# A counter of passed waits on VectorE in a kernel of two transformer layers

## The chip, the cores and the metric

The kernel runs on one core of a Trainium2 chip. The metric is the device time of one execution in microseconds (us), median of three runs. The engines are TensorE (PE in the profile; PEld is its weight load), VectorE (DVE), ScalarE (ACT), GpSimd (POOL) and the DMA queues, of which SyncE (SP) issues most.

## The reference

Sixteen sequences of 256 rows of 128 channels pass through four sublayers. Each is `x = x + layernorm(sublayer(layernorm(x)))`:

```python
x = x + _layernorm(_L0_attn_ref(_layernorm(x), ...))  # a long convolution with a complex decaying filter
x = x + _layernorm(_L0_ffn_ref(_layernorm(x), ...))   # top 2 of 8 experts (softmax router) + a shared expert
x = x + _layernorm(_L1_attn_ref(_layernorm(x), ...))  # 16 heads of 64, causal, ALiBi, 2 null keys, l2-normed q and k
x = x + _layernorm(_L1_ffn_ref(_layernorm(x), ...))   # top 2 of 4 experts: SwiGLU, two MLPs, a small normed block
```

Mean and variance of rows are thus needed at ten or so places of a sequence, and each router needs the two largest of its logits:

```python
topk_probs, topk_idx = jax.lax.top_k(router_probs, TOP_K)   # L0_ffn
rw, sel = jax.lax.top_k(logits, K)                          # L1_ffn
```

## The kernel before

The sixteen sequences are worked in eight groups of two, that is four tiles of 128 rows. All data stay in SBUF; weights are loaded and folded in an opening. The work is a software pipeline: the letters in a step's name say which sublayer it belongs to, `e_` and the first part of `l_` the convolution, the rest of `l_` the first expert layer, `a_` the attention, `f_` the second expert layer. One round of the pipeline works on four groups at once (`MIDDLE`: e of group i+2, l of i+1, a of i, f of i-1), before it stand `PROLOGUE` and `FIRST`, behind it the shorter `LAST_L`, `LAST_A` and `LAST_F`. In each table the order of the steps on each engine is written out by hand, and each engine runs its list strictly in that order.

Engines meet through semaphores. A `Signal` is a semaphore that rises by a fixed number in each group, and `s.at(g, n)` is the value after n steps of group g. Every instruction that makes something raises its signal, and whoever needs it waits for the value; that holds inside one engine too: a DVE instruction that reads what the DVE instruction before it has written waits for its semaphore.

The steps that the text speaks of:

- `stats` and `half_stats` (L1297 and L1318) take mean and variance of four or two tiles on DVE: `bn_stats` for each tile, a wait for them, `bn_aggr` for each tile, a wait, and one `tensor_scalar` that makes `norm.var`. POOL then makes the reciprocal root (`root` L840, `half_root` L847: `rooted`), and DVE's `apply` or `half_apply` (L1310, L1332) normalizes the tiles; `half_residual` (L1338) adds the residual. The norms are n_x, n_y (convolution), n_l (router input), n_d (after the experts), n_a (before attention), n_o (after it), n_m (before the second expert layer), n_c, n_c2 (inside it), n_f (after it) and n_z (the same for the last group).
- `l_pick` (L1405) and `f_route` (L1559) copy the router's logits, take the eight largest of each row (`max`), wait, and take their places (`max_index`, in the trace MATCH_VALUE_LOAD and FIND_INDEX8).
- `l_xl` (L1386) makes `xaT_lo`, the low part of the attention's input, from PE's transposes; PE's first projection `a_m` (L1655 to L1657) needs it. In front of it PE runs `f_clock` (L1974), five matmuls whose result nobody reads.
- `l_cT` (PE, L1777) turns the routing coefficients; it also waits for `f_out` (DVE, L1607) of an earlier group, the weighted sum over the experts, which DVE runs behind `l_route`, `l_pick` and `l_coef`.
- `f_ceT` (PE, L1662) turns `ce_rows`, which DVE has normalized with n_c (L1310).
- `weigh_biases` (POOL, L900 and L904) and `conv_gains` (POOL, L856) are large element-wise operations of POOL.

A semaphore that is only counted up and that nobody waits for exists once already, in `keep_x2` on POOL: `pool.sem_inc(pool_passed, 1)` (L865). On DVE the opening has increments as instructions of their own, behind waits for DVE's own last result: `dve.sem_inc(z_made, 1)` (L1188), `dve.sem_inc(gain_made, 1)` (L1210) and others. There the helper `link` gives each instruction an increment of `made` and puts a wait for it behind it.

Of the kernel before, what the change touches and what calls it, by code (L numbers as in the profile page):

```python
# [228 lines left out]
def program(nc, a, out):  # L229
# [24 lines left out]
    with ExitStack() as ctx:  # L254
# [3 lines left out]
        def sem(name):  # L258
            return ctx.enter_context(nc.semaphore(name))
# [218 lines left out]


        last_stored = sem("last_stored")  # L480
        pool_passed = sem("pool_passed")

        x_loaded = signal("x_loaded", 16)
# [88 lines left out]
        def ce_and_logits(b):  # L572
            return bank[6 + b][:, 0:2 * (P + 8)].rearrange("p (t d) -> p t d", t=2)
# [55 lines left out]
        def tiles(h):  # L629
            return range(2 * h, 2 * h + 2)  # L630
# [539 lines left out]
        def _(dve):  # L1170
# [126 lines left out]
            def stats(norm, g, tile):  # L1297
                s = norm.steps
                for t in range(T):
                    V.bn_stats(norm.six[:, t, :], tile(t)).then_inc(s.sem, 1)  # L1300
                dve.wait_ge(s.sem, s.at(g, 4))
                for t in range(T):
                    V.bn_aggr(norm.mv[:, t, :], norm.six[:, t, :]).then_inc(s.sem, 1)
                dve.wait_ge(s.sem, s.at(g, 8))
                V.tensor_scalar(norm.var[:], norm.mv[:, :, 1], norm.scale, norm.add, ALU.mult, ALU.add).then_inc(s.sem, 1)
# [12 lines left out]
            def half_stats(norm, g, h, tile):  # L1318
                s = norm.steps[h]
                for t in tiles(h):  # L1320
                    V.bn_stats(norm.six[:, t, :], tile(t)).then_inc(s.sem, 1)
                dve.wait_ge(s.sem, s.at(g, 2))
                for t in tiles(h):
                    V.bn_aggr(norm.mv[:, t, :], norm.six[:, t, :]).then_inc(s.sem, 1)
                dve.wait_ge(s.sem, s.at(g, 4))
                V.tensor_scalar(norm.var[:, 2 * h:2 * h + 2], norm.mv[:, 2 * h:2 * h + 2, 1], norm.scale, norm.add,
                                ALU.mult, ALU.add).then_inc(s.sem, 1)
# [13 lines left out]
            def e_stats(g):  # L1341
                if first(g):
                    dve.wait_ge(x0_loaded, 16)
                else:
                    dve.wait_ge(x_loaded.sem, x_loaded.at(g))
                stats(n_x, g, lambda t: xin[:, t, :])
# [25 lines left out]
            def l_turn2(g):  # L1372
                dve.wait_ge(l_turned.sem, l_turned.at(g, 2))
                stats(n_y, g, lambda t: bank[3][:, t * P:(t + 1) * P])

            def l_res(g):
                apply(n_y, g, xn, lambda t: bank[3][:, t * P:(t + 1) * P])
                add_residual(n_y, g, x1, xn, xin)
                dve.wait_ge(n_y.steps.sem, n_y.steps.at(g))
                stats(n_l, g, lambda t: x1[:, t, :])  # L1380
# [24 lines left out]
            def l_pick_(g):  # L1405
                s = l_pick
                dve.wait_ge(s.sem, s.at(g, 1))
                for t in range(T):
                    V.max(top0[:, t, :], logit0[:, t, :]).then_inc(s.sem, 1)
                dve.wait_ge(s.sem, s.at(g, 1 + T))  # L1410
                for t in range(T):
                    V.max_index(idx0[:, t, :], top0[:, t, :], logit0[:, t, :]).then_inc(s.sem, 1)
                V.tensor_tensor(exp0[:], top0[:], top0[:, :, 0:1].to_broadcast([P, T, 8]), ALU.subtract).then_inc(s.sem, 1)
# [35 lines left out]
            def l_down_(g, h):  # L1449
                dve.wait_ge(l_down.sem, l_down.at(g, 2 * h + 2))  # L1450
                half_stats(n_d, g, h, lambda t: bank[4 + h][:, t * P:(t + 1) * P])
# [8 lines left out]
            def a_stats(g, h):  # L1460
                dve.wait_ge(n_d.steps[h].sem, n_d.steps[h].at(g))
                half_stats(n_a, g, h, lambda t: x2n[:, t, :])
# [57 lines left out]
            def a_out_(g, h):  # L1520
                dve.wait_ge(a_out.sem, a_out.at(g, h + 1))
                half_stats(n_o, g, h, lambda t: out_bank(g, h)[:, t * P:(t + 1) * P])
# [36 lines left out]
            def f_route(g):  # L1559
                s = f_pick  # L1560
                for b in range(2):
                    dve.wait_ge(f_ce.sem, f_ce.at(g, b + 1))
                    V.tensor_tensor(logit1[:, 2 * b:2 * b + 2, :], ce_and_logits(b)[:, :, P:P + 8],
                                    b1_router[:].unsqueeze(1).to_broadcast([P, 2, 8]), ALU.add).then_inc(s.sem, 1)
                dve.wait_ge(s.sem, s.at(g, 2))
                for t in range(T):
                    V.max(top1[:, t, :], logit1[:, t, :]).then_inc(s.sem, 1)
                dve.wait_ge(s.sem, s.at(g, 2 + T))
                for t in range(T):
                    V.max_index(idx1[:, t, :], top1[:, t, :], logit1[:, t, :]).then_inc(s.sem, 1)  # L1570
                V.tensor_tensor(gap1[:], top1[:, :, 1], top1[:, :, 0], ALU.subtract).then_inc(s.sem, 1)
# [58 lines left out]
            def f_end(g):  # L1630
# [6 lines left out]
                "s_null": s_null, "s_kvlo": s_kvlo, "s_qlo": s_qlo, "s_v2": s_v2, "s_bias": s_bias, "s_split": s_split,  # L1637
                "e_stats": e_stats, "e_apply": e_apply, "e_scan": e_scan, "e_sum": e_sum, "l_turn2": l_turn2, "l_res": l_res,
                "l_norm": l_norm, "l_turn3": l_turn3, "l_ct": l_cT, "l_xl": l_xl, "l_route": l_route, "l_pick": l_pick_, "l_coef": l_coef, "l_hg": l_hg_, "l_hu": l_hu_,
                "l_hc": l_hc_, "l_dstats": l_down_, "l_end": l_end, "l_astats": a_stats, "l_aapply": a_apply,  # L1640
                "a_null": a_null, "a_ss": a_sums, "a_u": a_units,
                "a_nexp": a_nexp_, "a_nt": null_low, "a_mix": a_mixes, "a_o": a_out_, "a_end": a_end,
                "f_stats": f_stats, "f_apply": f_apply, "f_route": f_route, "f_pick": f_pick_, "f_ce": f_ce_,
                "f_ce_apply": f_ce_apply, "f_ce2": f_ce2, "f_ce2_apply": f_ce2_apply, "f_hid": f_sw, "f_out": f_out,
                "f_end_stats": f_end_stats, "f_end": f_end, "f_gen": f_gen_, "f_zstats": z_stats, "f_zend": z_end,
# [437 lines left out]
def build(nc, inputs):  # L2083

    arrays, args = {}, {}
    for name, value in inputs.items():
        v = np.ascontiguousarray(value)
        arrays[f"in_{name}"] = v
        args[name] = nc.dram_tensor(f"in_{name}", v.shape, mybir.dt.from_np(v.dtype), kind="ExternalInput").ap()
    out = nc.dram_tensor("out_0", inputs["L0_attn_x"].shape, F32, kind="ExternalOutput").ap()  # L2090
    program(nc, args, out)
    return arrays
# [10 lines left out]
```

## Time and profile before

| | |
|---|---|
| median of three runs | 1025.73 us (1025.63 to 1029.7) |
| the profiled execution | 1029.7 us, span 1028.0 us |
| granted TensorE clock, mean | 0.978 |
| PE busy | 953.4 us (93%) |
| DVE busy | 790.3 us (77%), 2393 instructions |
| ACT busy | 614.6 us (60%) |
| POOL busy | 580.4 us (56%) |
| DMA | 11 GB/s on average |

The span goes from the first instruction of the program to its last. Busy time is time with an instruction running, and semaphore instructions are not counted in it. Times in the timeline are microseconds from the span's start.

### The profile page before, as it was taken

The numbers are of one execution on the slowest core, as the hardware profiler recorded it, in microseconds if no ns is written. First come the engines' busy times: TensorE is split into PE (matmuls) and PEld (weight loads), VectorE is DVE, ScalarE is ACT, GpSimd is POOL, SyncE is SP. The second block draws the span as 40 slices with busy tenths as digits, with TensorE's granted clock in tenths as the row PEclk, the third lists the DMA queues.
The fourth block names the chain that finished last, engine by engine and source line by source line (L and its number), as shares of the span: only waits on it lengthen the run. The fifth ranks groups of instructions, "written<-read, shape, count | busy, mean of one in ns | idle before, by whom it ended". The sixth has DMA issues, their size and how long they took to land. (4 is left out here: it accounts for less than half of the span.)

```text
span 1028.0 us, 22028 instructions
## 1 busy us (share of the span) xinstructions
PE 953.4 (93%) x8405; PEld 737.5 (72%) x8405; DVE 790.3 (77%) x2393; ACT 614.6 (60%) x1288; POOL 580.4 (56%) x570
## 2 busy tenths in 40 slices
PE   0887899999999999999999999999999999999987
PEld 0566778687686868678686867768686777768755
DVE  6887578879788787878888796887788776873576
ACT  4418773876558653886648673785537674586621
POOL 4227563766558463764747573665648644755631
PEclk9969899999999999999999999999999999999999
DMA  6300000000000000000000000000000000000000
GB/s 161 91 0 11 2 2 2 1 11 1 13 1 1 12 12 2 1 11 2 13 1 1 12 12 2 1 11 2 12 1 1 1 12 2 1 1 2 12 1 11
DMA packets 22090, 11.52 MB, mean 11 GB/s; under 512 B 7648, under 2 KB 21344, under 8 KB 21856
## 3 DMA queue, kind: packets, MB, share of 16 engines
q1 hardware_dynamic: 18272, 8.86, 3.2%
q10 hardware_dynamic: 3712, 1.25, 0.5%
q8 instruction: 67, 1.10, 0.5%
q14 instruction: 39, 0.32, 0.1%
HBM read 8.00 MB, written 2.10 MB: 10 GB/s over the span
## 5 line engine op out<-in xcount | busy, mean ns | idle before, releaser
L870 POOL TENSOR_TENSOR rnorm<-sumsq,minus_half 128x16 f32<-128x16 f32 x64 | 187.3, 2949 | 16.4 <-DVE sumsq L1485 15.2
L878 POOL TENSOR_TENSOR unit<-unit,causal 128x256 f32<-128x256 f32 x128 | 93.2, 751 | 93.0 <-ACT unit L1120 93.0
L878 POOL TENSOR_TENSOR square<-square,causal 128x256 f32<-128x256 f32 x128 | 97.7, 786 | 69.0 <-ACT square L1120 68.5
L1883 PE MATMUL bank<-qT,kT 64*128 64x256 f32 x512 | 95.2, 389 | 0.0
L1479 DVE TENSOR_REDUCE sumsq<-square 128x16 f32<-128x1024 f32 x64 | 77.9, 1217 | 15.1 <-ACT square L1067 14.0
L1114 ACT ACTIVATE square<-bank,bias_k,rnorm 128x256 f32<-128x256 f32 x128 | 65.8, 571 | 38.5 <-PE bank L1883 38.5
L1889 PE MATMUL bank<-qT,kT 64*128 64x128 f32 x512 | 84.0, 284 | 2.3 <-ACT unit L1120 1.5
L1889 PEld LDWEIGHTS bank<-qT,kT 64*128 64x128 f32 x512 | 71.0, 186 | 17.7 <-issue 6.5
L1060 ACT ACTIVATE unit<-bank 128x512 f32<-128x512 f32 x128 | 72.3, 602 | 16.5 <-PE bank L1657 14.3
L1662 PEld LDWEIGHTS bank<-ident,unit 128*128 128x128 f32 x520 | 61.0, 144 | 24.7 <-DVE unit L1491 11.6
L1662 PE MATMUL bank<-ident,unit 128*128 128x128 f32 x520 | 70.4, 281 | 7.4 <-DVE unit L1491 6.0
L1046 ACT ACTIVATE xaT_hi<-bank 128x256 fp32r<-128x256 f32 x16 | 5.4, 382 | 117.1 <-PE bank L1814 117.1
L1067 ACT ACTIVATE square<-unit 128x512 f32<-128x512 f32 x128 | 72.8, 630 | 0.0
L1114 ACT ACTIVATE unit<-bank,bias_k,rnorm 128x256 f32<-128x256 f32 x96 | 51.5, 575 | 33.2 <-PE bank L1883 33.2
L1883 PEld LDWEIGHTS bank<-qT,kT 64*128 64x128 f32 x512 | 68.7, 186 | 0.7
L1510 DVE STREAM_TRANSPOSE mixed<-bank 128x256 f32<-128x256 f32 x64 | 28.5, 446 | 49.7 <-PE bank L1922 49.6
L1655 PE MATMUL bank<-w_kv_hi,xaT_hi 128*128 128x512 f32 x128 | 61.1, 478 | 1.4 <-ACT unit L1060 0.4
L1959 PE MATMUL bank<-w_out,qT 128*128 128x128 f32 x512 | 58.8, 275 | 0.9 <-DVE qT L1517 0.9
L1959 PEld LDWEIGHTS bank<-w_out,qT 128*128 128x128 f32 x512 | 57.9, 192 | 1.5 <-DVE qT L1517 1.4
L1120 ACT ACTIVATE unit<-bank,bias_k,rnorm 128x128 f32<-128x128 f32 x128 | 52.9, 480 | 0.0
L1120 ACT ACTIVATE square<-bank,bias_k,rnorm 128x128 f32<-128x128 f32 x128 | 52.5, 474 | 0.0
L1517 DVE TENSOR_TENSOR qT<-bank,mixed 128x512 f32<-128x512 f32 x64 | 44.3, 692 | 10.2 <-PE bank L1922 9.0
(385 smaller groups left out, 2753.8 us busy)
## 6 DMA issues: line engine op xcount, KB each, us to landing
xin<-in_L_attn_x SPq DMA_DIRECT2D x7, 256.0 KB, 2.8
out<-x SPq DMA_DIRECT2D x7, 256.0 KB, 2.3
square<-in_L_attn_w_kv SPq DMA_DIRECT2D x1, 1024.0 KB, 7.6
w_sw<-in_L_ffn_sw_w SPq DMA_DIRECT2D x3, 256.0 KB, 5.3
unit<-in_L_attn_w_q SPq DMA_DIRECT2D x1, 512.0 KB, 6.0
w_out<-in_L_attn_w_out SPq DMA_DIRECT2D x8, 64.0 KB, 2.1
w_ml<-in_L_ffn_ml_w SPq DMA_DIRECT2D x2, 256.0 KB, 5.6
xin<-in_L_attn_x ACTq DMA_DIRECT2D x1, 256.0 KB, 3.2
```

Source lines behind the costliest of these rows:

```text
L870: pool.tensor_tensor(rnorm[:, k, t, :], sumsq[:, t % 2, k, :], minus_half[:], ALU.pow).then_inc(a_root.sem, 1)
L878: m = pool.tensor_tensor(pd, pd, causal[:].unsqueeze(1).to_broadcast([P, 2, P]), ALU.mult)
L1060: act.activation(unit[:, t % 2, i, :], bank[n % 3][:], ACT.Copy).then_inc(a_took.sem, 1)
L1067: act.activation(square[:, k, :], unit[:, t % 2, k, :], ACT.Square).then_inc(a_sq.sem, 1)
L1114: last = act.activation(pr[:, j, 0:2, :], k0, ACT.Exp, bias=bias_k0[:, h:h + 1], scale=by)
L1120: last = act.activation(pr[:, j, 2, :], bank[2][:, 2 * P * s + P * j:2 * P * s + P * (j + 1)], ACT.Exp, bias=bias_k1[:, h:h + 1], scale=by)
L1479: V.tensor_reduce(sumsq[:, t % 2, k, :], square[:, 2 * k:2 * k + 2, :].rearrange("p j (h d) -> p (j h) d", d=DH), AX_X, ALU.add).then_inc( ...
L1655: mm(dst, left.hi, right.hi, start=True, stop=False)
L1662: last = nc.tensor.transpose(dst[:, t * P:(t + 1) * P], src(t), ident[:])
L1883: return mm(bank[s][:, 2 * P * i:2 * P * (i + 1)], kT[rs, p, 2 * P * b:2 * P * b + P], qT[rs, p, 2 * P * b:2 * P * (b + 1)], start=True, s ...
L1889: return mm(bank[2][:, 2 * P * s + P * i:2 * P * s + P * (i + 1)], kT[rs, p, ts], qT[rs, p, ts], start=True, stop=True)
L1959: last = mm(out_bank(g, h)[:, ts], outT[:, c, ts], w_out[:, c, :], start=(c == 0), stop=(c == 7))
```

## The change

A semaphore `dve_passed` is added. In `stats`, `half_stats`, `l_pick_` and `f_route`, after a wait of DVE for what DVE itself has just made, DVE raises it by one with an instruction of its own. Nothing waits for `dve_passed`. Nothing else changes.

```diff
         last_stored = sem("last_stored")
+        dve_passed = sem("dve_passed")
         pool_passed = sem("pool_passed")
...
                 dve.wait_ge(s.sem, s.at(g, 4))
+                dve.sem_inc(dve_passed, 1)
                 for t in range(T):
                     V.bn_aggr(norm.mv[:, t, :], norm.six[:, t, :]).then_inc(s.sem, 1)
...
                 dve.wait_ge(s.sem, s.at(g, 2))
+                dve.sem_inc(dve_passed, 1)
                 for t in tiles(h):
                     V.bn_aggr(norm.mv[:, t, :], norm.six[:, t, :]).then_inc(s.sem, 1)
...
             def l_pick_(g):
                 s = l_pick
                 dve.wait_ge(s.sem, s.at(g, 1))
+                dve.sem_inc(dve_passed, 1)
                 for t in range(T):
                     V.max(top0[:, t, :], logit0[:, t, :]).then_inc(s.sem, 1)
                 dve.wait_ge(s.sem, s.at(g, 1 + T))
+                dve.sem_inc(dve_passed, 1)
                 for t in range(T):
                     V.max_index(idx0[:, t, :], top0[:, t, :], logit0[:, t, :]).then_inc(s.sem, 1)
...
                 dve.wait_ge(s.sem, s.at(g, 2))
+                dve.sem_inc(dve_passed, 1)
                 for t in range(T):
                     V.max(top1[:, t, :], logit1[:, t, :]).then_inc(s.sem, 1)
                 dve.wait_ge(s.sem, s.at(g, 2 + T))
+                dve.sem_inc(dve_passed, 1)
                 for t in range(T):
                     V.max_index(idx1[:, t, :], top1[:, t, :], logit1[:, t, :]).then_inc(s.sem, 1)
```

## Rows read from the trace of the kernel before

**Rows 1.** The page's busy times: engine, us, share of the span, instructions.

```profile
PE 953.4 (93%) x8405; PEld 737.5 (72%) x8405; DVE 790.3 (77%) x2393; ACT 614.6 (60%) x1288; POOL 580.4 (56%) x570
```

**Rows 2.** Busy times by window, with the granted clock (PEclk), one group's middle and the tail.

```profile
core 0: us, PE busy (x) PEld busy (x) DVE busy (x) ACT busy (x) POOL busy (x), PEclk, DMA share, GB/s
...
200.00:240.00 40.00, 39.95 (x302) 32.80 (x304) 31.69 (x117) 29.56 (x60) 22.11 (x17) 1.00 0.03 8
...
984.00:1028.00 44.00, 32.41 (x174) 22.58 (x172) 29.75 (x107) 10.47 (x18) 12.99 (x13) 0.95 0.02 7
```

**Rows 3.** Timeline of DVE in the opening: start, duration, what [idle before].

```profile
7.37 0.15 DVE L1187 TENSOR_SCALAR vec<-vec 128x1 f32<-128x1 f32 x1
7.67 0.16 DVE L1189 TENSOR_TENSOR vec<-vec 128x1 f32<-128x1 f32 x1
...
10.96 0.17 DVE L1209 TENSOR_SCALAR vec<-vec 128x4 f32<-128x4 f32 x1
11.28 0.30 DVE L1198 TENSOR_SCALAR kT<-kT 128x257 f32<-128x257 f32 x1
```

**Rows 4.** PE's waits by releaser: us in total, times, longest.

```profile
PE bank L1655 <- DVE unit L1437: 12.8, 6, 2.5
```

**Rows 5.** Timeline of DVE and PE in front of group 2, 283 to 293 us.

```profile
283.80 0.50 DVE L1321 BATCH_NORM_STATS2 n_d_six<-bank 128x6 f32<-128x128 f32 x2 [0.47 <-PE bank L1806]
284.33 0.25 DVE L1324 BATCH_NORM_AGGREGATE n_d_mv<-n_d_six 128x2 f32<-128x6 f32 x2
...
285.59 0.73 DVE L1332 TENSOR_SCALAR xn<-bank,n_d_mv,n_d_rstd 128x128 f32<-128x128 f32 x2
286.43 0.43 DVE L1338 TENSOR_TENSOR x2n<-xn,x 128x256 f32<-128x256 f32 x1
...
288.68 1.12 DVE L1332 TENSOR_SCALAR ce_rows<-x2n,n_a_mv,n_a_rstd 128x128 f32<-128x128 f32 x4
...
290.95 0.50 DVE L1321 BATCH_NORM_STATS2 n_o_six<-bank 128x6 f32<-128x128 f32 x2
...
291.10 1.40 PE L1974 MATMUL bank<-w_kv_hi 128*128 128x512 f32 x5
...
291.48 0.25 DVE L1324 BATCH_NORM_AGGREGATE n_o_mv<-n_o_six 128x2 f32<-128x6 f32 x2
...
291.84 0.75 DVE L1386 TENSOR_TENSOR xaT_lo<-bank,xaT_hi 128x256 fp32r<-128x256 f32 x2
...
292.31 0.19 PEld L1655 LDWEIGHTS bank<-w_kv_hi,xaT_hi 128*128 128x128 f32 x1 [0.24 <-DVE xaT_lo L1386]
```

**Rows 6.** Timeline of the first router and what follows it, 345 to 353 us.

```profile
345.32 0.37 DVE L1409 MAX8 top<-logit 128x8 f32<-128x8 f32 x4
...
345.73 0.09 DVE L1412 MATCH_VALUE_LOAD idx<-top,logit 128x8 f32 x1
...
352.34 0.34 PEld L1777 LDWEIGHTS bank<-ident,pick 128*8 128x8 f32 x4 [0.40 <-issue]
```

**Rows 7.** Timeline, PE's wait in `f_ceT` of the sixth group.

```profile
787.12 0.42 PEld L1662 LDWEIGHTS bank<-ident,ce_rows 128*128 128x128 f32 x4 [0.53 <-DVE ce_rows L1310]
```

**Rows 8.** Timeline of the tail, 989 to 1001 us.

```profile
989.75 0.44 PE L1814 MATMUL bank<-ident,x4m 128*128 128x128 f32 x2 [0.54 <-DVE x4m L1332]
...
996.00 2.06 POOL L900 TENSOR_TENSOR conv<-row_out,pick 128x512 f32<-128x512 f32 x2
996.07 4.53 DVE L1310 TENSOR_SCALAR ce_rows<-ce_rows,n_c_mv,n_c_rstd 128x128 f32<-128x128 f32 x4
...
1000.65 0.66 PE L1662 MATMUL bank<-ident,ce_rows 128*128 128x128 f32 x4 [2.40 <-DVE ce_rows L1310]
```

**Rows 9.** Timelines of POOL and DVE beside each other, 256 to 260 us.

```profile
256.23 1.30 POOL L856 TENSOR_TENSOR conv<-conv,conv_a 128x512 f32<-128x512 f32 x1
...
256.91 3.33 DVE L1310 TENSOR_SCALAR x4m<-x4m,n_f_mv,n_f_rstd 128x128 f32<-128x128 f32 x4
```

## The prediction

> **What bounds the kernel now.** I read the page's busy table first: TensorE (PE) is busy for 93% of the span and VectorE (DVE) for 77% [rows 1]. Then the windows: between 200 and 240 us PE is busy for 39.95 of 40 us, at a granted clock of 1.00, while DVE has 8 us to spare; only the last 44 us are loose, PE busy for 32.41 [rows 2]. So in the body of the kernel PE is full: what delays PE at one place is not made up at the next, and what delays DVE costs nothing unless PE then waits for it. The question is therefore not how much DVE work is added but at which places PE starts an instruction the moment DVE's result is there. The PE rows of the timeline answer that, by the idle time in brackets and what ended it.
>
> **What the change does.** After a wait of DVE for its own last results it puts an increment of a new semaphore, `dve_passed`, that nobody waits for. No arithmetic, buffer, DMA or order changes. Sites, counted from the code and the written order: `stats` runs for n_x, n_y, n_l, n_c and n_c2 in all 8 groups and for n_f in 7, 47 times; `half_stats` 66 times (n_d, n_a, n_o, n_m twice in each of 8 groups, n_z twice); `l_pick` and `f_route` have two each in 8 groups, 32. That is 145.
>
> **Price of one site.** Today the wait belongs to the dependent instruction itself. In the timeline the first BATCH_NORM_STATS2 pair ends at 283.80 + 0.50 = 284.30 and the aggregate that waits for it starts at 284.33: 0.03 us [rows 5]. An increment of this form, a wait for DVE's own result and then an increment, is already in the opening: L1188 and L1210. L1187 ends at 7.37 + 0.15 = 7.52 and L1189 starts at 7.67; L1209 ends at 11.13 and L1198 starts at 11.28: 0.15 us both times [rows 3]. It is DVE's queue standing at it until the result is in, and only then taking up the instruction behind it, with the engine empty. So a site costs 0.15 - 0.03 = 0.12 us by figures rounded to 0.01; I take 0.11 us. The lower bound is a plain extra wait with no increment, L1336: L1332 ends at 285.59 + 0.73 = 286.32, L1338 starts at 286.43, so 0.11 - 0.03 = 0.08, I use 0.07 as the floor [rows 5]. All sites together lengthen DVE by 145 x 0.11 = 16 us, in 238 us of idle time.
>
> What stands behind the queue at a site: bn_aggr (two or four), the variance, then POOL's root that waits for the variance, and the DVE steps behind it. Each is late by what has gathered. The increment passes no other queue.
>
> The row shows the hold: 0.15 us against 0.03 [rows 3, 5]. The Trainium skill, "Perfetto Trace Analysis", section "Per-instruction lifecycle", says why: a datapath instruction goes into a wait queue and the sequencer moves on, whereas a sequencer-only instruction is waited for by the sequencer itself. The trace agrees, with those figures.
>
> **Where it reaches the end.** I go through PE's rows in order of time.
>
> The opening (up to 75 us) is a chain with little beside it. PE waits for n_y's and n_l's results at about 25 and 31 us, and DVE goes on to n_x and to n_d (second half) and both halves of n_a. Six of its ten sites lie on that chain: 6 x 0.11 = 0.66 us.
>
> The seams, one in front of each of groups 1 to 7, at 175, 292, 411, 528, 647, 766 and 882 us (seven times the five matmuls of L1974). In the one at 292 DVE runs without a pause from 283.80 to 292.59: statistics of n_d, of both halves of n_a, of both of n_o, and behind them `xaT_lo` (L1386). Aggregates stand at 284.33, 285.20, 287.41, 288.29 and 291.48: five sites, of which the first and the last are shown [rows 5]. PE fills the time before it with the five dummy matmuls of `f_clock` (L1974), which end at 292.50 by the model, and its first projection L1655 is released by `xaT_lo` [rows 5]. There is next to no margin. 5 x 0.11 = 0.55; off that 0.10 where DVE already waits inside the run (for POOL's root before 285.59, for PE before 290.95, both seen in that the next instruction does not overlap the one before) and 0.02 of margin: 0.43 a seam, 7 x 0.43 = 3.0 us.
>
> The routers. In `l_pick` two sites stand in a row (MAX8 at 345.32, MATCH_VALUE_LOAD at 345.73); behind them DVE runs `l_coef` and the `f_out` accumulations without a pause, and PE's `l_cT` (L1777) waits for the third of these, with 0.40 us idle in front of its weight load [rows 6]. 0.22 us in each of five groups, less some 0.07 that comes back where PE waits up to 2.5 us for `l_hg` behind ScalarE (six such waits, 12.8 us in all [rows 4]), whose chain has fewer sites: 5 x 0.15 = 0.75 us.
>
> The sixth group has a shorter order, and there `f_ceT` waits for DVE's `ce_rows`, 0.53 us of idle weight load at 787.12 [rows 7], behind three sites (two of `f_route`, one of n_c), and `l_turn3` behind two more (n_y, n_l) with about 0.2 us of room: 0.33 + 0.14 + 0.10 = 0.57 us.
>
> The tail (984 to 1028 us) is one chain through DVE: PE waits for x4m at 989.75 and for ce_rows at 1000.65 [rows 8]. Seven sites: n_o, n_m, two in `f_route`, n_c, and n_z twice; the two n_z runs partly cover each other and POOL's root. 0.6 us.
>
> Everything else, n_m, n_x, n_f, n_c2 and `f_route` in the middle groups, lies beside PE work and costs nothing while PE's queue holds more than about 0.3 us of work at that point, as it does between 292 and 345; without it each would cost 0.11.
>
> Sum: 0.66 + 3.0 + 0.75 + 0.57 + 0.6 = 5.6 us. The margins are read to 0.01 us, and one that is wider than read takes away and never adds, so I take 5.5. The profiled execution took 1029.7 us, its span 1028.0 and 1.7 around it; it would become 1035.2. The median of the three runs is 1025.73, 4 us below it, and the same 5.5 on it gives **1031.2 us**. With the floor of 0.07 the same places give 5.6 x 0.07 / 0.11, less the unchanged absorptions, about 2.9: 1028.6. The upper bound counts 0.12 a site and nothing absorbed (5 x 0.12 at seven seams, 0.24 at five routers, 6, 5 and 7 sites in the other three): 4.2 + 1.2 + 2.2 = 7.6: 1033.3.
>
> **The rivals.**
>
> Cheap or mostly covered. A site costs the 0.07 of the plain wait, or PE's dummy matmuls in fact have room for the run of DVE. For it: L1974 ends just when DVE does, so a few tenths of a us of room at each seam would hide the 3.0. Against it: PE is released by `xaT_lo` in the row. 1.0 to 4.3 us, say 1028.5.
>
> No cost at all. The increments do nothing to the time, because DVE has 23% idle and PE is the bound. Against it: the 0.15 us gaps behind L1187 and L1209. 1025.7. The Trainium skill, "VectorE: DVE Perf Modes", section "The DRAIN you can't avoid", speaks for it: eight copies with a semaphore after each took as long as with one at the end, "the semaphore costs nothing extra here". That is an increment carried by the instruction, not one of its own, and no run here shows that test; by that rule the time stays at 1025.7.
>
> Faster. DVE's apply of n_f (x4m, L1310) takes 3.33 us at 256.91, beside POOL's L856 from 256.23, where the like four of L1332 take 1.12 at 288.68 [rows 5, 9]. In five groups DVE loses 2.2 us that way. If the shift moved the apply behind POOL's two L856 (end 258.77), it would run in 1.1. That needs DVE to come 1.9 us later relative to POOL, and the shift there is 0.1 to 0.4, and the wait for PE behind it hangs mostly on ScalarE. If it came, PE's wait would shrink by up to 1.5 in five groups, 7.5 less 5.5 added: 1023.7.
>
> **Chances and range.** Full cost at the places named (4.3 to 7.6 us): 0.58. Cheap or covered: 0.27. No cost: 0.11. Faster: 0.04. Half a per cent, about what a measurement of this kernel can tell from no change, is 5.1 us, up to 1030.9; my forecast stands just over it, so its 0.58 divides into 0.46 above and 0.12 below; the cheap case gives 0.02 above. Slower 0.48, same 0.48, faster 0.04. The range goes from 1027.2 (the no-cost case and the lower part of the cheap one left out) to 1034.0 (the upper bound and 0.7 for the spread of runs).
>
> **What the changed profile would show.** Right: the aggregates, MAX8 and MATCH_VALUE_LOAD start 0.15 us behind their producers at all 145 sites; PE's first L1655 of each group has a longer idle in front of it, released by `xaT_lo`, about 0.4 us more; the group period grows by some 0.6 us from 117 to 119 us; the tail from 984 is 0.6 us longer; PE's and DVE's busy sums stay. Wrong: a gap of 0.10 or 0.03 at the sites (cheap or no cost); a seam where L1974 ends after `xaT_lo`; L1310 of x4m in 1.1 us instead of 3.3 (faster). The ce_rows apply at 996.07 takes 4.53 us beside POOL's L900 [rows 8]; both move together, so I expect it unchanged. If it changed, the tail would move by up to 3 us, which no term here holds.

## The result, and the profile after

The changed kernel took 1037.9 us, median of six runs (1037.05 to 1041.2). The kernel before, with six runs in all, took 1029.74 us (1025.63 to 1030.58). The ratio is 1.0098, with a 95% interval of 1.007 to 1.0126: slower by 0.7 to 1.3%, 8.2 us between the medians. I had forecast 5.5 us more, at 1031.2 us, with a range of 1027.2 to 1034.0. The direction was right; the time lies above the range.

The first lines of the page of the changed kernel, its span and busy times; the rows of before are [rows 1].

```profile
span 1038.8 us, 22173 instructions
PE 959.0 (92%) x8405; PEld 740.9 (71%) x8405; DVE 784.6 (76%) x2393; ACT 613.4 (59%) x1288; POOL 583.8 (56%) x570
```

The span is 10.8 us longer with the same numbers of engine instructions; the 145 more are the increments, which count as no busy time. But PE's busy time grew by 5.6 us on the same 8405 matmuls. Waiting for DVE cannot do that. It is the first sign of something that the forecast had no term for: in a second profile of this kernel, with less time at a low clock, PE's busy time is 953.4 us, as before. DVE's busy time fell by 5.7 us, where I had expected no change; the largest part lies in the `tensor_scalar` on `sumsq` (11.4 us in sum, 15.7 before), and its cause stays open.

**The holds.** The timeline in front of group 2, which answers to [rows 5]. Line numbers have moved: those around 1300 to 1400 by one to three, L1437 by five, and those of PE by seven, so that L1662 is here what was L1655, and L1669 what was L1662.

```profile
286.54 0.50 DVE L1323 BATCH_NORM_STATS2 n_d_six<-bank 128x6 f32<-128x128 f32 x2 [0.47 <-PE bank L1813]
287.18 0.25 DVE L1327 BATCH_NORM_AGGREGATE n_d_mv<-n_d_six 128x2 f32<-128x6 f32 x2
...
293.84 1.40 PE L1981 MATMUL bank<-w_kv_hi 128*128 128x512 f32 x5
294.02 0.49 DVE L1323 BATCH_NORM_STATS2 n_o_six<-bank 128x6 f32<-128x128 f32 x2
294.65 0.25 DVE L1327 BATCH_NORM_AGGREGATE n_o_mv<-n_o_six 128x2 f32<-128x6 f32 x2
...
295.01 0.75 DVE L1389 TENSOR_TENSOR xaT_lo<-bank,xaT_hi 128x256 fp32r<-128x256 f32 x2
295.48 0.19 PEld L1662 LDWEIGHTS bank<-w_kv_hi,xaT_hi 128*128 128x128 f32 x1 [0.67 <-DVE xaT_lo L1389]
295.48 0.50 PE L1662 MATMUL bank<-w_kv_hi,xaT_hi 128*128 128x512 f32 x1 [0.24 <-DVE xaT_lo L1389]
```

The statistics end at 286.54 + 0.50 = 287.04 and the aggregate starts at 287.18: 0.14 us, where it was 0.03. Read to the nanosecond, all 66 sites of the halves and all 47 of `stats` stand between 0.144 and 0.147 us. Of the 32 sites in the two routers 30 do too. One, in the opening, has no gap, because another instruction stands between it and what made its input, and one has 0.50 us (taken up below). The first projection of the group now finds PE idle, released by `xaT_lo`; PE's lateness against the kernel before grows by 0.42 us here. PE's waits by releaser (us in total, times, longest):

```profile
PE bank L1662 <- DVE unit L1442: 12.7, 6, 2.5
PE bank L1662 <- DVE xaT_lo L1389: 1.6, 7, 0.2
PE bank L1784 <- DVE x4m L1614: 1.5, 5, 0.6
```

The first line is [rows 4] again, all but unchanged. The second and the third are new: the seven seams and the five routers.

**The clock.** Three windows of the changed kernel, the first and the last behind an idle time of PE (columns as in [rows 2]):

```profile
385.00:388.40 3.40, 3.40 (x30) 2.37 (x33) 1.11 (x2) 0.19 (x1) 1.48 (x3) 0.50 0.00 0
504.40:507.80 3.40, 3.40 (x30) 2.42 (x33) 1.18 (x3) 0.18 (x1) 1.48 (x3) 0.51 0.02 5
...
1009.60:1013.00 3.40, 3.33 (x7) 1.92 (x8) 2.32 (x5) 1.09 (x2) 3.32 (x3) 0.50 0.00 0
```

There PE is granted the lower of its two levels, 1.2 in place of 2.4 GHz. Each of these stretches follows an idle time of PE of 2.5 to 2.7 us. At 504 us the timeline of PE shows both:

```profile
504.14 0.55 PE L1662 MATMUL bank<-xlT_hi,w_gate_hi 128*128 128x512 f32 x1 [2.48 <-DVE unit L1442]
504.49 0.63 PE L1663 MATMUL bank<-xlT_lo,w_gate_hi 128*128 128x512 f32 x1
504.92 0.63 PE L1664 MATMUL bank<-xlT_hi,w_gate_lo 128*128 128x512 f32 x1
```

A matmul of 512 columns takes 0.63 us; the same one two groups earlier, at 267 us and behind the same idle, takes 0.39. The kernel before has the same idle of 2.5 us at the same step, and no such stretch there; the experiments show its rows. Followed instruction by instruction, PE's lateness against before grows at this one place from 4.4 to 5.9 us.

In what follows I divide a run in two by what each run lists, its span and its mean granted clock: span x clock is its *time at full clock*, the rest is *lost to the clock*. In 52 runs of the kernel before the first is 1005.6 us on average (standard error 0.1) and the second 22.4 (0.4). Over these runs the span rises by 0.83 us for each us lost, with a correlation of 0.97: the 7 us by which runs of one kernel differ (1025.9 to 1033.0) go almost wholly with the clock. The slope is under 1, so a us "lost" by this count costs some 0.83 us, and the time at full clock comes out somewhat too low where more is lost.

| kernel | runs | mean time | time at full clock | lost to the clock |
|---|---|---|---|---|
| before | 52 | 1029.7 | 1005.6 | 22.4 |
| changed | 7 | 1039.0 | 1011.3 | 25.9 |
| only the 66 in `half_stats` | 8 | 1035.2 | 1009.5 | 23.9 |
| only the other 79 | 6 | 1035.1 | 1007.0 | 26.4 |
| increment in front of the wait | 10 | 1029.3 | 1005.2 | 22.3 |
| second wait without hold | 10 | 1030.0 | 1005.1 | 23.1 |
| a wait of its own, no increment | 10 | 1034.2 | 1008.7 | 23.7 |
| two increments | 5 | 1044.2 | 1018.4 | 24.0 |
| no increment, longer `f_clock` | 7 | 1034.0 | 1008.1 | 24.2 |
| before, `f_end` moved | 5 | 1012.8 | 994.8 | 16.2 |
| changed, `f_end` moved | 6 | 1020.0 | 1001.1 | 17.2 |
| before, `f_end` and `f_bias` moved | 4 | 1010.6 | 993.0 | 15.9 |

Standard errors are 0.1 to 0.5 us in the fourth column and 0.6 to 2.0 in the last, the line of before aside. So of the 9.3 us between the means, 5.7 are holds and 3.5 are clock by this count; with 0.83 us for each us lost it is 6.4 and 2.9.

### The profile page after: what moved, and what is told of

Read it like the earlier page. It is cut to its first block and busy times, and to the rows that moved or that the text cites. A ratio compares the mean times of both kernels' runs of the same rounds, so it can differ in the third digit from the quotient of the medians.

```text
span 1038.8 us, 22173 instructions
## 1 busy us (share of the span) xinstructions
PE 959.0 (92%) x8405; PEld 740.9 (71%) x8405; DVE 784.6 (76%) x2393; ACT 613.4 (59%) x1288; POOL 583.8 (56%) x570
## 5 line engine op out<-in xcount | busy, mean ns | idle before, releaser
L1669 PEld LDWEIGHTS bank<-ident,unit 128*128 128x128 f32 x520 | 60.6, 143 | 24.1 <-DVE unit L1496 11.1
L1669 PE MATMUL bank<-ident,unit 128*128 128x128 f32 x520 | 69.8, 279 | 7.1 <-DVE unit L1496 5.7
L1662 PE MATMUL bank<-w_kv_hi,xaT_hi 128*128 128x512 f32 x128 | 61.8, 483 | 3.0 <-DVE xaT_lo L1389 1.6
L1663 PE MATMUL bank<-w_kv_lo,xaT_hi 128*128 128x512 f32 x128 | 51.6, 403 | 0.0
```

Source lines behind the costliest of these rows:

```text
L1662: mm(dst, left.hi, right.hi, start=True, stop=False)
L1669: last = nc.tensor.transpose(dst[:, t * P:(t + 1) * P], src(t), ident[:])
```

## The experiments

**Part of the increments.** First those of `half_stats` alone, five of which lie in front of each seam.

```diff
# stats, l_pick_, f_route: as before; half_stats:
                 dve.wait_ge(s.sem, s.at(g, 2))
+                dve.sem_inc(dve_passed, 1)
```

> Only the 66 increments in the statistics of two tiles. Theory (a hold of 0.11 us at each site, paid only where PE waits for DVE, and the rest of the loss from additional stretches at a granted clock of 0.50): the seven seams stay at 0.42 us each, 2.9 us; 0.3 in the opening, 0.4 in the tail; 3.6 us, and 0 to 5 us from the clock, so 1029.3 to 1034 on 1025.7. PE's L1777 is not late. Rival (the loss spreads evenly over the sites): 66 of 145 of some 11 us, 5 us, with no place where it gathers.

Measured: 1034.58 us (1033.74 to 1037.41), ratio 1.0061 (1.0041 to 1.0081). PE's waits:

```profile
PE bank L1657 <- DVE xaT_lo L1388: 2.0, 7, 0.6
```

The seven seams are there (0.41 to 0.44 us each, one 0.76), the routers' L1784 is not among the waits. At full clock 3.9 us, near the 3.6 of the theory.

Then the other 79 alone, `stats`, `l_pick_` and `f_route`.

> Only the 79 other increments: statistics of four tiles and the two routers. Theory: nothing at the seams; 0.2 us at L1777 in five groups, 0.9 in the sixth group, 0.3 in the opening, 0.3 in the tail; 2.5 us, and 0 to 5 us from the clock. Rival (evenly over the sites): 79 of 145 of 11 us, 6 us.

Measured: 1035.23 us (1033.74 to 1037.05), ratio 1.0056 (1.0034 to 1.0078).

```profile
PE bank L1668 <- DVE ce_rows L1312: 3.2, 2, 2.7
...
PE bank L1783 <- DVE x4m L1613: 1.1, 5, 0.2
```

No wait for `xaT_lo` is left; the routers cost 0.2 us each. At full clock this kernel is only 1.4 us above before, less than the 2.5 that I expected (2.1 with the slope of 0.83), but it loses 4.0 us more to the clock. Judged by its time alone it would have spoken for the rival, a loss spread evenly over the sites; the waits and the time at full clock speak against it. At full clock the two parts add up, 3.9 + 1.4 = 5.3 against 5.7 for both; in time they do not, 5.5 + 5.4 against 9.3.

**What of a site costs.** First a kernel that was to have a wait of its own with no increment:

```diff
                 dve.wait_ge(s.sem, s.at(g, 2))
+                dve.wait_ge(pool_made, POOL_IDENT)
```

> At all 145 sites a second wait, for something that has long been there, in place of the increment. Theory: the hold is the queue standing at a wait of its own, so the gap is 0.10 us in place of 0.145, the seams cost 0.42 x 0.07/0.11 = 0.27 each, and the whole 3.5 us and 0 to 5 from the clock. Rival (it is the increment that costs): gaps of 0.03 and no change.

Measured: 1031.26 us (1025.47 to 1032.23), ratio 1.0007 (0.9985 to 1.0029). The edit missed its aim. The gaps in the trace are 0.034 us at the 113 sites of `stats` and `half_stats`: of two waits in a row the one written first stayed with the dependent instruction, and the other, for something long there, became the instruction of its own and held nothing. So what the run shows is that 145 more instructions on DVE's queue cost nothing in themselves.

The same with the two waits in the other order, so that the one for DVE's own result becomes the instruction of its own:

```diff
+                dve.wait_ge(pool_made, POOL_IDENT)
                 dve.wait_ge(s.sem, s.at(g, 2))
```

> At all 145 sites DVE's wait for its own result becomes an instruction of its own, with no increment, and the dependent instruction carries a wait for something long there. Theory: it is the hold of the queue that costs, 0.104 us between end and start in place of 0.034, so 0.07 a site; seams 5 x 0.07 less 0.1, 0.25 us each, 1.8 us, 3.3 us in all, and up to 5 us from the clock. Rival (the increment costs): no change in the time.

Measured: 1034.83 us (1030.69 to 1036.17), ratio 1.0044 (1.0026 to 1.0061), 3.1 us more at full clock. The last pair in front of group 2:

```profile
290.33 0.49 DVE L1323 BATCH_NORM_STATS2 n_o_six<-bank 128x6 f32<-128x128 f32 x2
290.93 0.25 DVE L1327 BATCH_NORM_AGGREGATE n_o_mv<-n_o_six 128x2 f32<-128x6 f32 x2
```

The gap is 0.11 us here and 0.103 over all sites. The hold alone costs 0.07, the increment behind it another 0.04, as the floor and the price of the forecast had it.

All increments in front of the wait:

```diff
+                dve.sem_inc(dve_passed, 1)
                 dve.wait_ge(s.sem, s.at(g, 2))
-                dve.sem_inc(dve_passed, 1)
```

> All 145 increments, each in front of its wait in place of behind it. Theory: the increment no longer stands between the wait and the instruction that needs it, the wait goes back to that instruction, the increment passes while DVE still computes; gap 0.03 us, seams as before, 1025.7 to 1030 like the kernel before. Rival (145 more instructions cost DVE time wherever they stand): the seams late by 0.4 us, about 11 us more.

Measured: 1029.47 us (1025.4 to 1031.92), ratio 1.0 (0.9978 to 1.0022). The gaps are back at 0.03 us:

```profile
288.18 0.50 DVE L1323 BATCH_NORM_STATS2 n_o_six<-bank 128x6 f32<-128x128 f32 x2
288.71 0.25 DVE L1327 BATCH_NORM_AGGREGATE n_o_mv<-n_o_six 128x2 f32<-128x6 f32 x2
```

The 145 instructions are all there, and they cost nothing. What costs is only where they stand: between a wait that has not come and the instruction that needs it.

Two increments at each site:

```diff
                 dve.sem_inc(dve_passed, 1)
+                dve.sem_inc(dve_passed, 1)
```

> Two increments of dve_passed in place of one at each of the 145 sites. Theory: the time of a site is the wait of DVE's queue for the result and the start behind it, and one more queue instruction adds only its own issue: if that is 0.04 us (0.145 less the 0.104 of the plain hold) a site costs 0.15, the seams 0.6 each, and the whole 8 us and the clock's share: 1039 to 1045. Rival (each increment costs the full 0.11 us): seams near 0.97, 12 us and the clock's share, 1043 to 1048.

Measured: 1045.68 us (1038.12 to 1046.68), ratio 1.0157 (1.0121 to 1.0192).

```profile
289.12 0.50 DVE L1324 BATCH_NORM_STATS2 n_o_six<-bank 128x6 f32<-128x128 f32 x2
289.85 0.25 DVE L1329 BATCH_NORM_AGGREGATE n_o_mv<-n_o_six 128x2 f32<-128x6 f32 x2 [0.24 <-DVE n_o_six L1324]
```

The gap is 0.24 us, so the second increment costs 0.10, not the 0.04 that I took from the difference between plain hold and increment. The rival was right on the price. A seam costs 0.9 to 1.0 us, and the whole 12.8 us at full clock: more than twice the single increment. At the seams that is because the part that DVE's own waits in the run absorb, 5 x 0.11 - 0.42 = 0.13 us, is absorbed only once. PE also waits for DVE at a place where one increment cost next to nothing:

```profile
PE bank L2004 <- DVE mixed L1610: 1.6, 6, 0.5
```

In the changed kernel that wait is 0.2 us, once. So what lies beside PE's work is free only up to a limit; how much of the 12.8 us comes from there was not worked out.

**What the shift does to the clock.** The kernel before with no increment, but seven matmuls in place of five in `f_clock`, so that each seam is longer by about what the holds cost there:

```diff
             def f_clock(g):
-                for _ in range(5):
+                for _ in range(7):
```

> The kernel before with no increment, and seven matmuls in place of five in f_clock: each seam is 2 x 0.234 us less the margin of 0.02 longer, 0.45 us, about what the five holds cost there. Theory: 7 x 0.45 = 3.2 us at the seams, and the body shifts against the granted clock as with the increments, so a 0.50 stretch at about 503 us, which the kernel before does not have, 1.5 us more: 4.7 us, 1030 to 1035. Rival (the clock has nothing to do with the shift): 3.2 us and the same stretches as before.

Measured: 1035.33 us (1030.08 to 1035.65), ratio 1.0044 (1.0023 to 1.0066). At full clock 2.5 us, and 0.39 us a seam in the trace, where I expected 0.45; the loss to the clock is 1.8 us above before's, with a standard error of 1, which by itself shows little. The profiled run has the additional stretch behind the third group's idle:

```profile
494.00:497.40 3.40, 0.89 (x8) 0.64 (x5) 3.19 (x7) 3.31 (x8) 2.46 (x4) 1.00 0.26 80
497.90:501.30 3.40, 3.40 (x43) 2.17 (x45) 1.43 (x4) 0.00 (x0) 0.90 (x2) 0.50 0.02 5
```

So this stretch can come with nothing added on DVE. The kernel adds PE work as well, so it is not a pure shift, and this is one profile.

Both kernels once more, each for a second profile:

> The kernel before once more, for its profile. Theory (the position of PE's idle times sets which of them are followed by a stretch at a granted clock of 0.50): the same body as in the first profile, stretches at about 382, 618 and 737 us, none at 503 and none at 263; only the opening differs, by up to 4 us. Rival (each idle of 2.5 us is followed by such a stretch by chance, 3 in 5): another set of places.

Measured: 1029.86 us. The same body as in the first profile: 0.50 behind the second, the fourth and the fifth of the five idle times of 2.5 us, and none behind the third:

```profile
382.20:385.60 3.40, 3.40 (x46) 2.17 (x48) 1.31 (x4) 0.00 (x0) 0.79 (x2) 0.51 0.02 5
501.60:505.00 3.40, 3.40 (x57) 2.53 (x50) 1.79 (x4) 0.57 (x2) 0.23 (x1) 1.00 0.00 0
```

```profile
499.92 0.50 PE L1655 MATMUL bank<-xlT_hi,w_gate_hi 128*128 128x512 f32 x1 [2.51 <-DVE unit L1437]
500.26 0.39 PE L1656 MATMUL bank<-xlT_lo,w_gate_hi 128*128 128x512 f32 x1
```

The same idle as at 504 us in the changed kernel, and behind it 0.39 us for the matmul that takes 0.63 there.

> The changed kernel once more, for its profile. Theory: stretches at 0.50 at about 385, 504, 624, 743 and 1010 us again, the seams late by 0.42 us each. Rival (chance): another set of places, the count between 1 and 5.

Measured: 1035.45 us. The opening had fewer slow stretches this time, the body came 6.8 us earlier, and here all five idle times have one behind them, and the tail's too:

```profile
260.80:264.20 3.40, 3.40 (x47) 2.14 (x49) 1.39 (x4) 0.00 (x0) 0.89 (x2) 0.50 0.00 0
...
499.70:503.10 3.40, 3.40 (x40) 2.15 (x42) 1.53 (x4) 0.00 (x0) 1.14 (x2) 0.51 0.02 5
```

So my theory holds in half: the two profiles of before, with the same opening, agree, but in the changed kernel the opening differs from run to run and moves the rest. Nor does the count of these stretches settle what a run loses: this one has six against before's three and yet loses less, 21.7 us against 22.6, because its opening had 17 us at 0.50, and the first profile's 34. Over all profiles, the stretches at 0.50 behind the idle of 2.5 us in the five middle groups and behind that in front of `f_ceT` in the last group:

| kernel, profile | group by group | last group |
|---|---|---|
| before, twice | - x - x x | - |
| increment in front; second wait without hold | - x - x x | x |
| `half_stats` only; longer `f_clock` | - x x x x | - |
| the other 79 only | - x x x - | x |
| changed, first | - x x x x | x |
| changed, second | x x x x x | x |
| a wait of its own | x x x - x | x |
| two increments | x - x - x (twice as long) | - |

The four profiles in which the groups are as long as before have none behind the third idle; the seven in which they are longer all have one. The idle is the same in all of them, so it does not by itself decide what follows.

**Without the idle times.** In front of the three steps that PE waits for, DVE runs `f_end`: the apply of n_f, slow beside POOL's L856 [rows 9], and a residual. In the five middle groups I moved `f_end` behind them.

```diff
 MIDDLE, "DVE":
-... l_hu.2 a_mix.2 f_end a_mix.3 l_hg.3 l_hu.3 l_hc.2 ...
+... l_hu.2 a_mix.2 a_mix.3 l_hg.3 l_hu.3 f_end l_hc.2 ...
```

> The kernel before, with DVE's f_end (the apply of n_f that takes 3.33 us beside POOL's L856, and the residual) moved behind a_mix.3, l_hg.3 and l_hu.3 in the five middle groups. Theory: the 2.5 us that PE stands idle in front of l_g.4 in each of these groups come from that apply; moved, the idle is under 0.5 us, and the stretches at a granted clock of 0.50 that follow at 382, 618 and 737 us are gone: 5 x 2 us plus 3 x 1.5 us faster, 1011 to 1018. Rival (the idle turns up again one wait later, since DVE's queue is as long as before): within 2 us of before, with an idle of PE in front of a_mix.4 or l_u.4.

Measured: 1012.12 us (1009.96 to 1015.73), ratio 0.9827 (0.98 to 0.9854) to before.

```profile
257.43 1.28 POOL L856 TENSOR_TENSOR conv<-conv,conv_b 128x512 f32<-128x512 f32 x1
...
260.51 0.68 DVE L1437 SCALAR_TENSOR_TENSOR unit<-mixed,bank 128x512 f32<-128x512 f32 x1
261.24 0.19 PEld L1655 LDWEIGHTS bank<-xlT_hi,w_gate_hi 128*128 128x128 f32 x1 [0.16 <-DVE unit L1437]
...
261.89 1.58 DVE L1310 TENSOR_SCALAR x4m<-x4m,n_f_mv,n_f_rstd 128x128 f32<-128x128 f32 x4
```

The apply takes 1.58 us in place of 3.33, and PE's idle of 2.5 us in front of L1655 is gone. So are all stretches at 0.50 between 116 and 986 us:

```profile
280.00:400.00 120.00, 118.93 (x1086) 93.57 (x1085) 99.03 (x311) 74.09 (x155) 72.35 (x66) 1.00 0.02 6
...
600.00:700.00 100.00, 98.76 (x839) 77.19 (x840) 80.38 (x262) 64.96 (x134) 60.48 (x52) 1.00 0.02 7
```

This is the version that beats both kernels: 10.8 us less at full clock and 6.2 less lost. Two things changed at once: the apply no longer runs beside L856, and the whole of `f_end`, 4.4 us with its residual, no longer stands in front of what PE waits for. No run parts the two.

The same move with all 145 increments:

> The same move with all 145 increments. Theory (5.7 us of holds, the rest clock): without the idles no group has a 0.50 stretch behind one, and the distance between this kernel and the one before with the move is 5 to 7 us in place of 8 to 11. Rival (the whole distance is holds): 8 to 11 us as without the move.

Measured: 1020.7 us (1013.34 to 1024.39), ratio 0.9899 (0.9864 to 0.9935) to before, so 0.9899 / 0.9827 = 1.0073 to the kernel above. At full clock 6.3 us, and 1.0 us more lost to the clock, with a standard error of 2.3, so the 3.5 us without the move is not excluded here. PE's waits show the holds where they were:

```profile
PE bank L1662 <- DVE xaT_lo L1389: 1.6, 7, 0.2
PE bank L1784 <- DVE x4m L1614: 1.4, 5, 0.6
```

In the two profiles the body has no stretch at 0.50, and PE's lateness against the kernel above grows from 1.2 to 6.2 us between 116 and 990 us through holds alone.

The last kernel takes up the same collision in the tail ([rows 8]): `f_end` moved as above, and POOL's `f_bias` behind `f_ce_apply` in the last group.

```diff
 LAST_F, "POOL":
-f_stats.1 f_ce f_bias f_ce_apply f_ce2 f_zstats.0 f_zstats.1
+f_stats.1 f_ce f_ce_apply f_bias f_ce2 f_zstats.0 f_zstats.1
```

> The kernel before with f_end moved (as in before_fend) and, for the last group, POOL's f_bias (L900, L904) put behind f_ce_apply, so that the apply of ce_rows no longer runs beside it. Theory: that apply takes 1.1 us in place of 4.5, PE's idle of 2.4 us in front of f_ceT and the stretch at 0.50 behind it are gone, 2.4 to 4 us below before_fend, 1008 to 1010. Rival (f_out now waits for f_bias, or f_ce2's root stands behind it): the same as before_fend, with a new idle of PE in front of f_out or f_ce2T.

Measured: 1010.82 us (1007.87 to 1013.06), ratio 0.9828 (0.9789 to 0.9868) to before.

```profile
976.92 1.12 DVE L1310 TENSOR_SCALAR ce_rows<-ce_rows,n_c_mv,n_c_rstd 128x128 f32<-128x128 f32 x4
...
978.96 0.60 PE L1662 MATMUL bank<-ident,ce_rows 128*128 128x128 f32 x4
...
980.76 2.05 POOL L900 TENSOR_TENSOR conv<-row_out,pick 128x512 f32<-128x512 f32 x2
```

The apply takes 1.12 us in place of 4.53, PE's 2.4 us in front of the transposes are gone, and so is the stretch at 0.50 behind them. At full clock it is 1.8 us below the kernel with `f_end` moved alone. The median stands just above the expected 1008 to 1010; in time the intervals of the two overlap, so a gain over it is not shown.

## Why the forecast was off, by its own steps

**The price of a site** was right: 0.145 us from end to start in place of 0.034, 0.11 more, and 0.07 with no increment.

**The places** were right: the seven seams, the five routers, the sixth group, the opening and the tail are all where PE's lateness grows outside the slow stretches; elsewhere it does not. For their sizes I compare two profiles that happen to share the course of the clock in the opening up to 100 us, the second one of the changed kernel and the one with the increments in front of the wait, and count only where PE's lateness grows without a stretch at 0.50:

| term | forecast | measured |
|---|---|---|
| opening | 0.66 | 1.0 |
| seven seams | 3.0 (0.43 each) | 3.0 (0.43 each) |
| five routers | 0.75 | 1.15 |
| sixth group | 0.57 | 0.9 |
| tail | 0.6 | 0.65 |
| sum | 5.6 | 6.7 |

By the mean over runs at full clock it is 5.7, and 6.4 with the slope of 0.83. The forecast's 5.5 us was about the right size for the holds, up to 1 us too low. One reading behind it was wrong: I put PE's waits of 2.5 us [rows 4] down to ScalarE, and the kernel with `f_end` moved shows that DVE's `f_end` stood in front of them. The routers are higher because of one of them, at L1784 in group 2, where PE was idle for 0.57 us and not 0.22. In `l_pick` of that group (profile of the changed kernel)

```profile
348.61 0.37 DVE L1413 MAX8 top<-logit 128x8 f32<-128x8 f32 x4
349.48 0.09 DVE L1417 MATCH_VALUE_LOAD idx<-top,logit 128x8 f32 x1 [0.50 <-DVE top L1413]
```

the second hold lasts 0.50 us in place of 0.15. It is the same one site in every profile with all 145 increments behind their waits, three in number, and 0.46 us in the one with a wait of its own; with the 79 alone, or with two increments, it is as short as the others. But there other sites are long: one of 0.50 us in the tail with the 79, and three of 0.59 to 0.61 us with two increments. With the 66 alone, and in every kernel without a hold, there is none. What it is stays open.

**The step that failed first** is the one that put the sum on a base: "the same 5.5 on it gives 1031.2 us". The 1025.73 of three runs is near the fast end of this kernel. Its mean over 52 runs is 1029.7, and the profiled execution, on which all the working rested, was with 1029.7 at that mean. 4.0 of the 6.7 us between 1031.2 and the measured 1037.9 are this step. I had seen both numbers 4 us apart and taken no account of the question which one a further run would resemble. From the profile the forecast was 1035.2, 2.7 us below the measured median.

**The second**, behind the rest, is a term that was missing: what the clock takes. I read the granted clock as 1.00 in the window from 200 to 240 us [rows 2] and treated it as given. It is not: the profile of before has three stretches at 0.50 between 380 and 741 us, each behind PE's idle of 2.5 us. The same idle is followed by such a stretch at one moment and not at another, and each costs 1.5 to 1.7 us. The changed kernel lost 3.5 us more to the clock on average (25.9 against 22.4, standard error 0.9), some 2.9 us of time. That this comes with the shift of the work and not with the increments themselves is supported and not proved: the third stretch stands in all seven profiles with longer groups, that of the longer `f_clock` among them, and in none of the other four; and with the idle times gone the body has none at all. How much of the 3.5 us comes from the body and how much from the opening no run tells.

**The rivals.** "No cost" fell with the gaps. The Trainium skill's rule that I weighed for it ("VectorE: DVE Perf Modes", section "The DRAIN you can't avoid") speaks of an increment that the instruction itself carries. No run here shows that case; the nearest, increments in front of the wait, cost nothing, 1.0 (0.9978 to 1.0022). "Cheap" fell too: the sites took 0.145 and not 0.103 us, each seam was late by 0.42, and the kernel that does have the price of a plain wait came out at 1.0044, 3.1 us at full clock. "Faster" fell as well: in the changed kernel the apply still takes 3.31 to 3.34 us in each of the five groups. It would not have run in 1.1 us behind L856 either: its last two parts started at 258.78 and 259.47 us, behind L856's end at 258.77, and still took 0.77 us each beside POOL's next operation, L878. That `f_end` is worth attacking was right: written further back in the order it gave 17 us, with the slowdown and the place in the queue not told apart.

**The range** took its upper end from 7.6 us of holds on 1025.73. On 1029.7 the same range would have been 1031.2 to 1038.0, and the measured 1037.9 would have lain just inside it, by luck: no term of that range is the clock's.

**What stays open:** what sets the slow stretches of the opening, which took 14 to 34 us at 0.50 in the profiles and move all that follows by up to 7 us between the two profiles of the changed kernel; what decides whether an idle of 2.5 us is followed by one; and the single long holds. How much of the 3.5 us another build of the same change would lose can't be told from this.

## What to carry to other kernels

An increment behind a wait for the engine's own last result takes the wait away from the instruction that needs it and stops the queue: 0.11 us a time on VectorE, and 0.07 for the wait alone as an instruction of its own. Put it in front of the wait, where it cost nothing (letting the producing instruction carry this second increment was not tried), and look only at the places where the bounding engine starts the moment that engine is done. Before a forecast of half a per cent, put the sum on the mean of many runs and not on three, look for idle times of PE that are followed by a low granted clock, and take the time lost to it as a quantity of its own: two kernels are compared by span x clock first, which errs by about a sixth of the difference in what they lose.

## What the runs showed of the hardware

- DVE's apply with a scalar per row takes three to four times as long with POOL operations on SBUF beside it: four of 128x128 took 4.53 us in place of 1.12 beside L900 and L904, and 3.33 beside L856 and L878. The Trainium skill ("SBUF — State Buffer", section "SBUF: two separate sides") calls it an exclusive lock on a port pair that the two share. The traces of before agree: every part of these applies that took over 0.6 us, 26 in one profile, ended 0.08 to 0.09 us behind the end of a POOL operation. Parted from them, the apply of n_f took 1.58 us and that of n_c 1.12.
- Behind PE's idle of 2.5 us in the middle groups a stretch at 1.2 GHz came in 39 of 55 cases over eleven profiles, and behind the idle of 2.4 to 3.0 us in the last group in 6 of 11. The same idle at another moment is followed by none.
- A wait for DVE's own result as an instruction of its own: 0.103 us from end to start; with an increment behind it 0.145; with two 0.244; carried by the dependent instruction 0.034. A second wait at the same places, for something that is long there, cost nothing: 1.0007 (0.9985 to 1.0029) with 145 of them. Of two waits in a row the one written first stayed with the instruction behind them.
